# A hybrid attention, expert and state-space layer: the batch loop written out, layer-norm statistics in four groups, and a later gate choice

## What is computed

```python
x = x + attn_a(layernorm(x), Wqkv, bqkv, Wo, bo)        # 16 heads of 32, masked softmax
x = x + ffn(layernorm(x), Wr, br, Wd, bd, Wu, bu)       # 8 experts of rank 16, the best 2 per token
x = x + attn_b(layernorm(x), W_in, conv_w, ..., W_out)  # state-space layer, 32 heads, 64 states
x = x + ffn(layernorm(x), Wr, br, Wd, bd, Wu, bu)

def ffn(x, ...):
    gates = softmax(x @ Wr + br + bonus)
    w = the two largest gates, divided by their sum, at their experts; 0 elsewhere
    h = relu(x @ Wd + bd)
    out = sum over experts of w * (h @ Wu + bu)
```

## Time and profile before

| what | us |
|---|---|
| median of 3 runs | 3033.44 (3031.54 to 3035.66) |
| profiled execution | 3038.13 |
| its span in the trace | 3036.2 |
| PE busy | 2832.4 |
| DVE busy | 1945.2 |
| ACT busy | 1203.6 |
| POOL busy | 878.3 |
| matmuls L768, L769, L770 with `uh`, `ul` on weights `win` | 622.3 + 601.1 + 600.1 |

### The profile page before, as it was taken

One profiled execution on the slowest core, in us unless ns is written; L12 is line 12 of the kernel. 1 busy time (PEld: TensorE's weight loads), 2 busy tenths in 40 slices (PEclk: granted clock), 3 DMA queues, 4 the chain that ended last, 5 costly groups with the idle time before them and its releaser, 6 DMA issues.

```text
span 3036.2 us, 59249 instructions
## 1 busy us (share of the span) xinstructions
PE 2832.4 (93%) x20484; PEld 2058.8 (68%) x20484; DVE 1945.2 (64%) x2948; ACT 1203.6 (40%) x1915; POOL 878.3 (29%) x1322
## 2 busy tenths in 40 slices
PE   3898999999998899999989989999999988999998
PEld 3655578777665568777765547877776555787776
DVE  2555566777745655777675547477776555757777
ACT  2244334444225434444323552444422454344442
POOL 3312212333222212333321231233333122123342
PEclk7999999999999999999999999999999999999999
DMA  9332111111233202111133220211123230211112
GB/s 350 94 70 66 34 46 41 49 50 49 85 80 67 50 22 56 44 51 47 42 99 77 50 50 22 65 51 47 40 71 92 50 81 19 58 48 47 45 46 81
DMA packets 163800, 192.20 MB, mean 63 GB/s; under 512 B 43962, under 2 KB 103994, under 8 KB 161786
## 3 DMA queue, kind: packets, MB, share of 16 engines
q1 hardware_dynamic: 155486, 175.31, 21.1%
q10 hardware_dynamic: 8096, 14.16, 1.5%
HBM read 106.99 MB, written 23.36 MB: 43 GB/s over the span
## 4 chain that ended last, share of the span: by engine, by line
PE 72%; DVE 15%; issue 5%; DMA 2%; ACT 2%; SPq 1%; POOL 1%; ACTq 1%; DVEq 0%; POOLq 0%
PE ps L768 16%; PE ps L769 15%; PE ps L770 15%; DVE mneg L1742 6%; PE ps L898 4%; PE ps L1163 4%; PE ps L955 3%; PE ps L937 2%; PE ps L1149 2%; PE ps L1172 2%; PE ps L893 2%; PE ps L1213 2%; DVE stats L1537 2%; DVE X L1593 1%; ACT PR L1363 1%
## 5 line engine op out<-in xcount | busy, mean ns | idle before, releaser
L768 PE MATMUL ps<-uh,win 128*128 128x512 f32 x1536 | 622.3, 405 | 0.6
L769 PE MATMUL ps<-ul,win 128*128 128x512 f32 x1536 | 601.1, 391 | 0.0
L770 PE MATMUL ps<-uh,win 128*128 128x512 f32 x1536 | 600.1, 391 | 0.0
L1742 DVE TENSOR_REDUCE mneg<-ps 128x1 f32<-128x128 f32 (+7 forms) x512 | 367.4, 753 | 346.9 <-PE ps L898 345.5
L1363 ACT ACTIVATE PR<-ps 128x1024 f32<-128x1024 f32 (+3 forms) x384 | 293.1, 807 | 309.9 <-PE ps L937 283.1
L2113 POOL TENSOR_SCALAR_AFFINE_SELECT LM<-LM 128x512 f32<-128x512 f32 x256 | 212.3, 840 | 501.4 <-ACT LM L1481 501.4
L768 PEld LDWEIGHTS ps<-uh,win 128*128 128x128 f32 x1536 | 288.5, 188 | 72.4 <-issue 9.5
L1856 DVE TENSOR_TENSOR LM<-ps,LM 128x512 f32<-128x512 f32 x256 | 170.3, 686 | 258.7 <-PE ps L1163 214.0
L770 PEld LDWEIGHTS ps<-uh,win 128*128 128x128 f32 x1536 | 288.4, 188 | 64.2
L769 PEld LDWEIGHTS ps<-ul,win 128*128 128x128 f32 x1536 | 289.1, 188 | 53.4
L955 PE MATMUL ps<-PR,V 128*32 128x512 f32 (+3 forms) x1536 | 286.6, 499 | 6.4 <-ACT OT L1373 3.8
(11 more groups left out here) (230 smaller groups left out, 5119.0 us busy)
## 6 DMA issues: line engine op xcount, KB each, us to landing
raw<-in_t SPq DMA_DIRECT2D x128, 256.0 KB, 2.8
QS<-EV SPq DMA_DIRECT2D x192, 128.0 KB, 2.6
KS<-EV SPq DMA_DIRECT2D x168, 128.0 KB, 2.6
in_t<-tiles ACTq DMA_DIRECT2D x10, 1024.0 KB, 9.5
XN<-in_L_attn_a_x_dram SPq DMA_DIRECT2D x40, 256.0 KB, 5.6
win_raw<-in_L_attn_a_Wqkv_dram SPq DMA_DIRECT2D x34, 256.0 KB, 3.4
win_raw<-in_t SPq DMA_DIRECT2D x32, 256.0 KB, 2.8
edec<-ed_t SPq DMA_DIRECT2D x512, 16.0 KB, 1.6
```

Source lines behind the costliest of these rows:

```text
L768: pe.matmul(dst, hi_l, hi_r, start=first, stop=False)
L769: pe.matmul(dst, hi_l, lo_r, start=False, stop=False)
L770: return pe.matmul(dst, lo_l, hi_r, start=False, stop=last)
L1742: dve.tensor_reduce(mneg[:, hh, t:t + 1], flat[:, off:off + (t + 1) * P], AX.X, ALU.max, negate=True).then_inc(a_max.sem, 1)
```

## The change

Four things are edited. (1) On PE, ACT, DVE and POOL the loop over the batches is a Python loop, so each of the four programs holds the four batches one after the other and its waits compare with constants; SP keeps its loop, and the inner loops over head pairs stay. (2) `LN_GROUPS` has four groups of two tiles instead of three (3, 3, 2); POOL's calls name the groups accordingly. Tiles 0 and 1 are centered ahead of addition 4. Their low parts and tile 2's centering come at t == `lows_behind`, 5 in general and 4 at the state-space join, where they came at 6. Tile 3 is centered ahead of the last tile's statistics. (3) The gate choice of tiles 0 to 3 stands behind the low part of tile 7, ahead of tile 6's logits. (4) `keep_awake(2, 8)` ahead of the second expert layer is `keep_awake(2, 3)`.

```diff
-LN_GROUPS = [(0, 3), (3, 6), (6, 8)]
+LN_GROUPS = [(0, 2), (2, 4), (4, 6), (6, 8)]
...
-            with pe.Fori(0, NB) as b:
+            for b in range(NB):
...
                 w_add.wait(pe, b * 2 + 1, 3)
-                keep_awake(2, 8)
+                keep_awake(2, 3)
                 first_turns(b * 4 + 3)
...
-            with act.Fori(0, NB) as b:
+            for b in range(NB):
...
             def by_tile(n, take, last_added, src):
 
+                center(n, 3, src)
                 last_added()
                 tile_stats(n, TT - 1, src)
-                center(n, 3, src)
...
-            def add_tiles(n, product, added, bank, stats_of, src, loaded=None, banks=4):
+            def add_tiles(n, product, added, bank, stats_of, src, loaded=None, banks=4, lows_behind=HALF + 1):
 
                 for t in range(TT):
+                    if t == HALF:
+                        first_tiles(stats_of, src)
                     product.wait(dve, n, t + 1)
...
                         tile_stats(stats_of, t - 1, src)
-                        if t == HALF:
-                            first_tiles(stats_of, src)
-                        elif t == HALF + 2:
+                        if t == lows_behind:
                             turned_tiles(stats_of, src)
...
                 def behind(t):
+                    if t == HALF + 2:
+                        gate_choice(0)
                     logits(t)
...
-                    elif t == HALF + 1:
-                        gate_choice(0)
                     elif t == HALF + 2:
                         gate_weights(0)
...
-            with dve.Fori(0, NB) as b:
+            for b in range(NB):
...
-                add_tiles(b * 2 + 1, w_pe, w_add, 0, b * 4 + 3, X, banks=TT)
+                add_tiles(b * 2 + 1, w_pe, w_add, 0, b * 4 + 3, X, banks=TT, lows_behind=HALF)
...
-            inverse_roots(0, (0, 1))
+            inverse_roots(0, (0, 1, 2))
             value_lo(0)
             group_lo(0)
-            with pool.Fori(0, NB) as b:
-                inverse_roots(b * 4, (2,))
+            for b in range(NB):
+                inverse_roots(b * 4, (3,))
...
-                inverse_roots(b * 4 + 4, (0, 1))
+                inverse_roots(b * 4 + 4, (0, 1, 2))
```

## The result

| kernel | median, us | ratio to the kernel before (95% interval) |
|---|---|---|
| before | 3034.56 (7 runs) | |
| changed | 3047.33 (7 runs, 3042.74 to 3056.74) | 1.0041 (1.0028 to 1.0053) |

The account below looks back on a forecast made before the run. PE's work plus the stretches where it stands still or runs slowly was taken to bound the kernel. Joins, turns and smaller terms summed to +0.3 us, the clock added 9.1: 3033.44 became 3043, range 3022 to 3052.

Parts of the forecast that it names:

- Attention join: After attention, four times: DVE waits for ScalarE's copy ahead of addition 6, PE starts 0.6 later; +2.3 us in all.
- The group's 0.46: At every join: four groups cost DVE 2.40 us where three cost 1.94, so 0.46 more work.
- The step that PE's early start buys nothing: State-space and first expert joins: PE starts sooner but waits for the third low part; +1.8 us for each kind.
- Gate choice: Eight expert layers: PE's wait of 0.93 moves from the last logits to the up-projections; +0.1 each, +0.8 us in all.
- Batch turns: Three turns: value product 1.5 us sooner, DVE's issue wait gives 0.76, first projection 2.26 sooner; -6.8 us in all.
- The page on instruction fetch: Batch turns: by the skill's branch-stall rule alone each turn gives back PE's whole branch, -10.5 us, 3.7 under the sum.
- Register operations: On DVE: 928 operations of 40 ns leave most waits, running ahead of unmet waits; -0.5 us, upper bound 5.6.
- the third case: Rival, chance 0.23: faster, 3025 us (3018 to 3028), as the issue path was worth more; constant waits save 5.6.
- Start and tail: Program's first statistics and the turns: DVE's added group may reach PE once more; two times 0.46, about +0.9 us.
- The clock: Half-rate PE stretches land on needed work at ten attention, state-space and first expert joins, 0.91 each; +9.1 us (0 to 17).
- Case 2: Rival, chance 0.22: PE's new waits at the joins bring no clock cost; only +0.3 left, 3034 us (3028 to 3037).
- case 4: Rival, chance 0.05: longer programs make the inner head-pair loops stall like the batch branch, 20 us or more; 3060 and above.

Follow-up runs that it names:

- e6: Changed kernel with the low parts of tiles 0 and 1 back behind addition 6 in every join; ratio 1.0017 to the kernel before, +5.2 us.
- e1: Kernel before with only the batch loops of PE, ACT, DVE and POOL written out; ratio 0.9983 to the kernel before, -5.2 us.
- e4: Kernel before with the four groups alone, all else at its old place; ratio 1.0013 to the kernel before, +3.9 us.
- e8: Changed kernel with PE's batch loop put back, the other three written out; ratio 1.0050 to the kernel before, +15.2 us.
- e5: Changed kernel with unread matmuls in the two gaps at the state-space join; ratio 1.0027 to the kernel before, +8.2 us.
- e3: Kernel before with only the gate choice of tiles 0 to 3 moved behind tile 7's low part; ratio 0.9993, -2.1 us.
- e9: Changed kernel with DVE's batch loop put back, the other three written out; ratio 1.0092 to the kernel before, +27.9 us.
- e10: e7 with four unread matmuls in each of PE's two waits at the batch turns; ratio 0.9965 to the kernel before, -10.6 us.
- e7: Kernel before with loops written out and early low parts at the batch turns alone; ratio 0.9979 to the kernel before, -6.4 us.

## Why the prediction was right, and where it was not

**Attention join.** Right in mechanism: the wait of DVE was forecast with 2.5 and measured with 2.57, the loss with 0.57 for the order and 0.1 for the choice. By the pairing the third logits start 0.58 later, and the first up-projection 0.75. e6, with the low parts late, loses nothing here. The written-out loops alone give 0.3 at this join (e1), which is not seen on top of this in the changed kernel; why, no run shows.

**First expert and state-space joins.** The group's 0.46 is what e4 measured (0.40 to 0.48). The step that PE's early start buys nothing held. Beside it the early low parts cost nothing but clock: 24.81 us in e8 against 24.8 in e6 at the first expert join, and with PE kept busy at the state-space join (e5) 0.13 to 0.61. The term that was too small is the clock, below.

**Gate choice.** Forecast +0.8 in eight layers. The mechanism, a wait moved from the last logits to the up-projections, is in the rows (1.24 and no 0.93), and in e3 the first up-projection starts 0.1 to 0.2 late in all eight. The first expert layers keep about 0.1 of it, as forecast, in the two batches where it can be read. In the second ones it is gone by the last up-projection. The median of e3, -2.1 (up to +0.6), doesn't show the 0.8.

**Batch turns.** Forecast 1.5 sooner for the value product and 2.26 for the projection. Against the same addition the value product came 1.55 sooner (822.94 + 3.38 - 824.77) and the projection 2.2. That 3.38 is what the turn starts late by. At the first projection the three turns give 2.20, 2.24 and 2.53, 7.0 against the forecast 6.8. What the forecast missed is that one turn of three would fall on the low clock behind it and keep 0.66 only. The split of the gain was partly luck: I gave 0.76 to the end of DVE's stall as if this were its worth for any order. By e1 its worth alone is 0.2 to 0.6 a turn. By e9 it is 2.2 a turn at the first projection once the low parts are early, for then no wait for PE stands behind it, and 3.6 with the low stretches that follow. That PE's branch has no sum of its own held in both orders (e8).

**The page on instruction fetch.** The Trainium skill's rule ("Runtime: NRT & Kernel Launch", section on instruction fetch mechanics), that a taken branch out of the prefetched window stalls for a fetch, agrees with e8's branch of 3.5 us. The time by that rule alone, the whole branch given back at each turn, did not come: e8 loses nothing at the turns by it.

**Register operations.** I took 0.5; e1 shows 2.2 in eight joins, though that run writes out the loops and so doesn't part the register operations from the rest. This was part of the third case, whose 5.6 was too much.

**Start and tail.** The 0.9 taken for them has no run of its own. In the changed kernel the first attention join starts 0.24 late.

**The clock.** Forecast 9.1 us at ten places of 0.91. This is the term that was mis-sized, and that the total is near is partly luck: the places were not as forecast. None of the four attention joins shows the low clock, though PE waits there. All four first expert joins show it, two of them as before. The two added ones differ by 0.95 from the others (1.74 and 1.72 against 0.80 and 0.77), which looks like the forecast price of 0.91. But the stretch costs 1.33 in each of the four (changed kernel against e8), less 0.95 in the two where the kernel before paid it too, 3.4 in all. A state-space join costs 1.6 by e5 against the 0.91 taken: the third logits, at half rate, are what DVE waits for next. One turn cost 1.6, and a stretch at 1707 us in an attention layer some 1.8, which nothing in the prediction covered. So 3.4 + 6.6 + 1.6 + 1.8 is 13.4, where 9.1 was said; for the rest 13.0 - 13.4 leaves -0.4, where +0.3 was said.

Case 2 (gaps without a clock cost) is out by e5, case 4 by the row of the inner branches, which are as short as before:

```profile
L1225 PEldq COMPARE_BRANCH  x28: 76/208/243, 519.8 to 2953.6; - x28
```

Left open: what decides in which batch a stretch falls low. It differs between kernels at places that an edit has not touched, and runs of one kernel differ by it too: the changed kernel's seven runs spread over 14 us, those of the kernel before over 4 beside them, and over 12 on another chip.

## What to carry to other kernels

Handing a consumer its first pieces earlier is worth nothing if the third comes when it did, and it can cost. It can make the engine that hands over wait for a copy (the attention join), and it cuts the consumer's wait into pieces between its tiles, and if a half-rate stretch follows them, it falls on work that others wait for (the two other joins). Read which piece is last, move only where the wait for the first piece is what ends last (here the turn, not the joins), and fill the waits that remain with unread matmuls. A stall's worth is not a property of the stall; before removing one, or an order that hides one, look for the wait that stands behind it, and test the two edits apart and together.

## What the runs showed of the hardware

The same matmul stream, 12 matmuls of 256 columns in the third logits, ran at 1.00 or at about 0.50 behind different work of PE: with 30 unread matmuls and one wait of 0.73 ahead it was 1.00, with waits of 2.24 and 1.79 it was 0.52. But at the attention join, waits of 2.6 us in DVE and 1.23 in PE were not followed by the low clock before that join's end, in any kernel here. And at the first expert join of batch 3 the same waits of PE, 1.69 us the longest, were followed by a clock of 0.51 in the changed kernel and of 1.00 in e8, which made 1.33 us. Lastly, keeping PE busy at the turns was followed by the loss of low stretches more than 200 us later, at places with the same instructions (e10 against e7), which I had not expected and can't explain.
